# State-space chunk loop on one core: softplus summed by matmuls, five instead of six items read out by GpSimd, preparation one chunk sooner

## The reference

```python
dt = jax.nn.softplus(jnp.einsum('blr,dr->bld', dt, dt_proj_w) + dt_proj_b)
A = -jnp.exp(A_log)
def step(h, inputs):
    dt_t, B_t, C_t, u_t = inputs
    dA = jnp.exp(dt_t[:, :, None] * A)
    h = dA * h + (dt_t * u_t)[:, :, None] * B_t[:, None, :]
    y = jnp.einsum('bdn,bn->bd', h, C_t)
    return (h, y)
y = ys.transpose(1, 0, 2) + u * D
y = y * jax.nn.silu(z)
```

## Time and profile before

| | |
|---|---|
| time, median of 3 runs | 1969.87 us (1968.13 to 1972.08) |
| profiled execution | 1968.55 us, of which span 1966.8 us |
| share busy over the span | PE 79%, DVE 66%, POOL 62%, ACT 50% |
| loop of layer 0, first to last gate | 71.5 to 594.1 us |
| loop of layer 1, first to last gate | 1108.8 to 1631.7 us |

### The profile page before, as it was taken

One profiled execution on the slowest core, in us unless ns is written; L12 is line 12 of the kernel. 1 busy time (PEld: TensorE's weight loads), 2 busy tenths in 40 slices (PEclk: granted clock), 3 DMA queues, 4 the chain that ended last, 5 costly groups with the idle time before them and its releaser, 6 DMA issues. The chain is left out here.

```text
span 1966.8 us, 28246 instructions
## 1 busy us (share of the span) xinstructions
PE 1561.5 (79%) x6220; PEld 925.5 (47%) x6221; DVE 1294.5 (66%) x2306; ACT 991.5 (50%) x1594; POOL 1220.5 (62%) x1179
## 2 busy tenths in 40 slices
PE   5677777777778999999982677777777777699996
PEld 2222222222227998889971222222222226666664
DVE  5799999999997431111106699999999997510112
ACT  4777677777772311222223677676777772122112
POOL 2699999999992001444435599999999992033310
PEclk7799999999995899999995799999999996599997
DMA  5778777777783304777756887777777871523323
GB/s 137 190 171 185 170 174 170 175 175 169 171 185 109 126 27 135 228 216 222 222 161 143 198 179 171 170 176 174 168 173 178 179 171 36 193 81 122 116 66 105
DMA packets 104482, 310.86 MB, mean 158 GB/s; under 512 B 19388, under 2 KB 74508, under 8 KB 93068
## 3 DMA queue, kind: packets, MB, share of 16 engines
q1 hardware_dynamic: 91896, 291.72, 59.4%
q0 software_dynamic: 12544, 18.63, 4.1%
HBM read 258.83 MB, written 51.45 MB: 158 GB/s over the span
## 5 line engine op out<-in xcount | busy, mean ns | idle before, releaser
L696 POOL TENSOR_TENSOR mamba_dbu<-mamba_rep 128x462 f32<-128x462 f32 x640 | 676.5, 1084 | 43.6 <-DMA mamba_rep<-dt_rows 36.5
L508 PE MATMUL mamba_ysum<-mamba_hc,all_sel 128*128 128x462 f32 x800 | 421.7, 610 | 239.3 <-DVE mamba_hc L801 238.6
L622 ACT ACTIVATE mamba_state<-mamba_rep,all_m_acol 128x462 f32<-128x462 f32 x640 | 388.8, 638 | 244.5 <-DVE mamba_last L816 243.5
L819 DVE TENSOR_TENSOR_SCAN mamba_state<-mamba_state,mamba_carry,mamba_dbu 128x462 f32<-128x462 f32 x400 | 454.0, 1171 | 7.5 <-ACT mamba_state L622 7.5
L508 PEld LDWEIGHTS mamba_ysum<-mamba_hc,all_sel 128*128 128x128 f32 x800 | 127.3, 194 | 519.5 <-DVE mamba_hc L801 501.5
L691 POOL TENSOR_TENSOR mamba_hcp<-mamba_last,mamba_rep 128x462 f32<-128x462 f32 x240 | 266.4, 1110 | 45.3 <-DVE mamba_last L816 38.0
L816 DVE TENSOR_TENSOR_SCAN mamba_last<-mamba_state,mamba_last,mamba_dbu 128x462 f32<-128x462 f32 x240 | 279.5, 1164 | 14.8 <-POOL mamba_dbu L696 7.4
L801 DVE TENSOR_TENSOR mamba_hc<-mamba_state,mamba_rep 128x462 f32<-128x462 f32 x400 | 247.1, 619 | 0.0
L503 PE MATMUL mamba_ysum<-mamba_hcp,all_sel 128*128 128x462 f32 x480 | 238.2, 579 | 0.0
L1439 DVE TENSOR_TENSOR moe_h<-moe_sg,moe_up 128x512 f32<-128x512 f32 x62 | 42.6, 687 | 282.4 <-PE moe_up L1248 275.9
L1209 POOL DMA_INDIRECT token_rows<-moe_eo,moe_row x44 | 69.8, 1586 | 134.1 <-ACT moe_eo L1382 119.2
...
## 6 DMA issues: line engine op xcount, KB each, us to landing
...
```

What stands on the lines that cost most here:

```text
L508: nc.tensor.matmul(ysum[:, 0:TC], sel[:, i // NM, :], hc[:, n % HCD, :], start=False, stop=end).then_inc(hc_summed, 1)
L622: nc.scalar.activation(state[:, STATE_BANK[i], 0:TC], rep[:, par * REP_ROWS + i // NM, :], ACT.Exp, scale=m["acol"][:, i:i + 1]).then_inc( ...
L696: pool.tensor_tensor(dbu[:, i % 4, :], rep[:, first + NG + i // NM, :], rep[:, first + 2 * NG + i % NM, :], ALU.mult).then_inc(dbu_ready, 1)
L819: nc.vector.tensor_tensor_scan(bank, bank, dbu[:, i % 4, :], carry[:, i:i + 1], ALU.mult, ALU.add).then_inc(scan_done, 1)
```

## The change

- **Items.** ON_POOL is (1, 4, 7, 10, 13), five items instead of six. DVE's eleven are item 0 and the pairs (2,3), (5,6), (8,9), (11,12), (14,15). A pair is read out together, after the scan of the item that follows it; where both items have neighbouring rows of C it is one instruction of 924 columns (four of five pairs). The copy to `carry` stands ahead of the read-out. `hc` has seven slots, `hcp` five. ACT's exp waits for a pair's read-out instead of its copy.
- **Softplus.** ACT writes ln(1+e) to SBUF (into `ab`). PE adds ln + relu - rr into PSUM with three matmuls by the identity and a negated identity (`prep_add`), and ACT copies the sum to `dd` (`prep_dd`). DVE keeps `prep_rr` only, now behind item 10.
- **Sooner.** POOL's product for chunk k+2 stands behind its item 15; `store_dt` of k+2 follows in the same pass of SP's loop; `dt_rows` in DRAM is doubled. PE's u and z are for chunk k+3.
- **Loops.** DVE's and POOL's chunk loops are Python loops: 20 chunks of instructions written out per layer, with constants for slots and for most semaphore values.
- **Gate** (AT_Y) stands behind the third scan instead of the first.

The diff, cut to its core:

```diff
-ON_POOL = (0, 3, 6, 8, 11, 13)
+ON_POOL = (1, 4, 7, 10, 13)
-SUM_ORDER = tuple(sorted(range(ITEMS), key=lambda i: i if i in ON_DVE else min(i + 2.5, ITEMS - 1.5)))
-HCP = 3
-HCD = 5
+LAST_OF = tuple(i + 1 if FIRST[i] else i for i in range(ITEMS))
+SUM_ORDER = tuple(sorted(range(ITEMS), key=lambda i: LAST_OF[i] + 2 if i in ON_DVE else i + 3.1))
+HCP = 5
+HC_SLOT = (0, 1, 2, 3, 4, 5, 6, 1, 2, 3, 4)
-AT_SILU, AT_EXP, AT_ONE, AT_LN, AT_BC, AT_DT, AT_DTU, AT_Y = 6, 10, 11, 15, 13, 5, 3, 0
+AT_SILU, AT_EXP, AT_ONE, AT_BC, AT_LN, AT_U, AT_DTU, AT_Y, AT_RR, AT_ADD, AT_DD = 3, 6, 7, 8, 9, 12, 15, 2, 10, 9, 15
...
+            def prep_add(k):
+                pe.wait_ge(front_act, START + ACTS * k + A_LN)
+                nc.tensor.matmul(front[:, 1, 0:TC], g["ident"][:, :], ab[:, :], start=True, stop=False)
+                nc.tensor.matmul(front[:, 1, 0:TC], g["ident"][:, :], rx[:, :], start=False, stop=False)
+                pe.wait_ge(front_dve, START + DVES * k + D_R)
+                nc.tensor.matmul(front[:, 1, 0:TC], nident[:, :], rr[:, :], start=False, stop=True).then_inc(front_mm, 1)
...
+                if s == AT_U1:
+                    pe.wait_ge(minus_ready, 1)
+                    prep_add(0)
                     prep_u(1)
...
+            def prep_dd(k):
+                act.wait_ge(front_mm, START + MMS * k + MM_ADD)
+                if not (isinstance(k, int) and k == 0):
+                    act.wait_ge(dt_stored, 16 * NG * k)
+                nc.scalar.activation(dd[:, 0, :], front[:, 1, 0:TC], ACT.Copy).then_inc(front_act, 1)
...
-                        elif FIRST[free]:
-                            act.wait_ge(carry_done, START + COPIES[-1] * k + COPIES[free] - COPIES[-1] * before)
                         else:
-                            act.wait_ge(hc_ready, START + ND * k + ON_DVE.index(free) + 1 - ND * before)
+                            act.wait_ge(hc_ready, START + ND * k + ON_DVE.index(LAST_OF[free]) + 1 - ND * before)
...
-            with pool.Fori(0, NCH // 2) as pair:
+            prep(1)
+            for pair in range(NCH // 2):
...
                         if i == AT_DTU:
-                            prep(k + 1)
+                            prep(k + 2)
...
-            with dve.Fori(0, B) as b:
+            for b in range(B):
...
+                        end = LAST_OF[i] + 1
+                        n, width, bank = ON_DVE.index(i), end - i, STATE_BANK[i]
+                        dve.wait_ge(scan_done, START + ITEMS * k + end)
+                        nc.vector.tensor_copy(carry[:, i:end], state[:, bank:bank + width, TC - 1]).then_inc(carry_done, 1)
+                        dve.wait_ge(hc_summed, START + ND * k + n + width - HC_GAP[n + width - 1])
+                        at_once = width if i % NM + width <= NM else 1
+                        for w in range(0, width, at_once):
+                            nc.vector.tensor_tensor(hc[:, HC_SLOT[n + w]:HC_SLOT[n + w] + at_once, :],
+                                                    state[:, bank + w:bank + w + at_once, 0:TC],
+                                                    rep[:, c_rows + (i + w) % NM:c_rows + (i + w) % NM + at_once, :], ALU.mult).then_inc(hc_ready, at_once)
...
-                    read_out(ITEMS - 1)
-                    prep_rr(k + 2)
-                    prep_dt(k + 2)
+                        if i == AT_RR:
+                            prep_rr(k + 2)
+                        if i - 1 in ON_DVE and not FIRST[i - 1]:
+                            read_out(i - 2 if SECOND[i - 1] else i - 1)
+                    read_out(ITEMS - 2 if SECOND[ITEMS - 1] else ITEMS - 1)
```

103 lines of the change are left out of this document (46 added, 57 removed).

## The result

The changed kernel takes 2025.9 us (median of 4, 2022.0 to 2027.4) against 1970.8 for the kernel before on the same chip: a ratio of 1.028 (1.026 to 1.030). The profiled execution took 2027.1 us, its span 2024.6. The forecast was 1974 with a range of 1944 to 1998, so both were too low.

A forecast was written before the change was run, and what follows sets the result against it. It took three rings per chunk (DVE 24.6, POOL chain 25.3, ACT 25.4 us) plus clock falls in two of five chunks, mean 26.0; gain 984.0 - 38 x 26.0 = -4, so 1972.6 profiled, 1974 us median, range 1944 to 1998.

The forecast's parts named there:

- The chain over POOL: Pair (8,9) read-out, PE sums and additions, ACT copy, POOL product, next first scan: 25.3 us per chunk.
- DVE's 24.63 us: DVE's own work in a chunk after the change, the loop's pace if nothing else were late.
- ACT's ring of 25.4: Pair (14,15) read-out, ACT's exp 2 to exp 10, then DVE's scan 10 to that pair again: 25.4 us.
- The plain chunk of 25.4: Chunk without a clock fall, set by the longest of three rings (24.6, 25.3, 25.4): 25.4 us.
- The start-ups: Earlier preparation delays the store before each loop, 2.9 us in layer 0 and 4.6 in layer 1: +7.5 us.
- The price of a fall: Two PE operations slowed when TensorE's clock falls at the new pause: 1.57 us, chunk 26.9 instead of 25.4.
- The pause of 2.1 to 2.3 us: PE's unbroken idle stretch between item 7's sum and the pair (8,9), in every chunk.
- the share of chunks with a fall: Chunks in which TensorE's clock falls at PE's pause: two in five, giving a mean chunk of 26.0 us.
- falls in most chunks: Rival: clock falls at PE's new pause in most chunks; chunk up to 26.9 us, 1985 to 2008 us, chance 0.17.
- The end of a loop: Last chunk of each loop, from its first scan to the last gate: 28.1 us.
- DVE becomes the only bound: Rival: rings of ACT and POOL shorter, no falls; chunk 24.9 us, 1928 to 1948 us, chance 0.10.
- Code comes late: Rival: DVE's written-out instructions arrive late; 0.1 to 0.25 us a chunk, hidden or +4 to +9; no chance of its own.

The follow-up runs named there:

- add7: Changed kernel with rr behind item 7 instead of 10 and PE's three additions behind item 7 instead of 9; 1924.1 us, ratio 0.977.
- split: Changed kernel with PE's u and z behind the 11th sum and the two additions not needing rr ahead of sum 8; ratio 0.989.
- fill3: Changed kernel with u and z behind the 11th sum and three overwritten matmuls of ab in PE's pause before pair (8,9); ratio 0.992.
- u10: Changed kernel with one number changed: PE computes u and z behind its 11th sum instead of its 13th; ratio 1.013.
- fill: Changed kernel with 14 small matmuls, results unused, in PE's pause between the sums of items 7 and 8; 1963.5 us, ratio 0.997.
- before_flat: Kernel before with only the hardware chunk loops of DVE and POOL written out as Python loops; ratio 0.992.
- ring2: Changed kernel with two more passes of ab through PE ahead of the three additions, each overwritten; ratio 1.033.
- add_dve9_u10: Changed kernel with the two softplus operations back on DVE, rr behind scan 9, and u and z behind the 11th sum; ratio 1.016.

## Why the prediction was wrong, by its own steps

**Right.** The chain over POOL: each of its links is in the trace, in order, with the wait at scan 0 at its end, and with the fall its ring is 27.01, the forecast's 25.3 plus 1.71. PE's steps at full clock, the double read-out (1.03 from start to start, forecast 1.02), DVE's 24.63 us (add7, 24.88 with a wait of 0.19) and ACT's ring of 25.4 (split, 25.36). The plain chunk of 25.4 is right only where u and z stand two sums sooner (fill3, 25.5). The start-ups: first gate 76.6 (forecast about 77), between the loops 520.4 (about 522). The price of a fall, 1.57, was 1.7. The pause of 2.1 to 2.3 us is that of u10 (2.26); in the changed kernel it is 2.80, since the read-out of the pair stands behind the wait ahead of scan 10.

**The step that failed first, and cost most,** is the share of chunks with a fall. The forecast took "two in five, nearer to the row", from nine falls in 38 at a shorter pause. It was 38 in 38: 38 x 0.9 (26.9 for 26.0) is 34 us of the 54.5 by which the profiled execution is above the forecast of 1972.6. The forecast said "the far end is every chunk", gave falls in most chunks 0.17, and had no reason to prefer the near end but that it was the row at hand. That the new pause is longer and stands in every chunk was a reason to prefer the far one.

**The ring that was missing.** The forecast summed three rings: DVE's own, ACT's, and the one over the additions and POOL. It had no term for u and z on PE and the wait of silu for them, which it put at nothing without a reason. That is a fourth ring, and the longest: with the fall 27.41 against 27.01. It is too long at the full clock as well (fill, 25.85 where the forecast has 25.4), so the lateness of z is no effect of the falls alone; the fall only comes on top. Of 27.34 for 26.9, 0.14 is the fall (1.71 for 1.57) and the rest the wait of 0.4 ahead of scan 10 (together 0.1 more than is needed): 38 x 0.44 = 17 us. u10 shows it from the other side: with z two sums sooner, chunks with a fall and without that wait are 26.7 to 26.9.

**The end of a loop** comes on top: the last gate is 26.3 us behind the one before, not 24.2, for the same two reasons. Twice 2.1 is 4 us. Then 34 + 17 + 4 - 2 (start-ups) + 1 (the tail) is 54, of 54.5.

**The rivals.** "Falls in most chunks" was the right one. Its mechanism was as described, its price short by the missing ring. "DVE becomes the only bound" is what add7 is, and it is not far: two numbers in the table decide. "Code comes late" was wrong: written-out loops gave 0.31 us a chunk (before_flat), about what their branches were counted for. That gain is inside the changed kernel's time.

**Left open.** What decides whether the clock falls. The pause alone doesn't: 2.80 us gave a fall in each chunk of the changed kernel and only in the first few of each loop in ring2, 2.26 us gave one in 30 of u10's 38 chunks and none in eight. The runs don't tell why the share was 38 of 38. Nor was each part of the change tried by itself: what the eleventh read-out, the paired read-outs and the product for chunk k+2 behind item 15 are worth is not shown. With the additions back on VectorE and z sooner, what is left is at 1.016 (add_dve9_u10).
